# A decoder layer on one core: the last 12 steps' maxima sent by transfers, the rows of ones written by GpSimd, the heads turned by transposes, the last batch normalised out of the bank

## The reference

```python
x = _layernorm(x + attn(x))          # causal self-attention with folded low-rank weights
x = _layernorm(x + xattn(x, ctx))    # queries from x; keys and values from [ctx, x], causal over x
x = _layernorm(x + ffn(x))           # 128 -> 64 units, each with a 16-wide relu layer of its own -> 128
# in each attention, per head:
dots = q @ k.T / sqrt(8);  attn = softmax(where(mask, dots, -inf));  out = attn @ v
```

## Time and profile before

| | |
|---|---|
| median of 3 runs | 268.14 us (268.12 to 269.94) |
| profiled execution, its own time | 270.45 us |
| span of the profiled execution | 268.7 us |
| busy PE / DVE / ACT / POOL | 91% / 72% / 72% / 39% |
| mean granted TensorE clock | 0.937 of full |

### The profile page before, as it was taken

How to read it: one execution, slowest core, us unless ns; L and a number is a source line. 1 busy time by engine, 2 the same in 40 slices (tenths; PEclk the granted TensorE clock), 3 DMA queues, 4 the chain that set the end, 5 groups by cost and what they waited for, 6 DMA issues and landing times.

```text
span 268.7 us, 7856 instructions
## 1 busy us (share of the span) xinstructions
PE 243.7 (91%) x3037; PEld 150.3 (56%) x3037; DVE 193.8 (72%) x422; ACT 193.1 (72%) x412; POOL 106.0 (39%) x286
## 2 busy tenths in 40 slices
PE   8989998979999998899999999999999999998680
PEld 5676676758785654354555546544446455556440
DVE  1899991956868998979878897699878776544101
ACT  3263888867879786689987888789977987682131
POOL 7203597595745253721125222523321540412301
PEclk9997999979999997899999999999999997979757
DMA  4917888793997746370000000253000000000000
GB/s 103 372 60 146 245 143 122 241 175 58 285 157 155 115 133 104 118 119 3 4 0 2 2 0 4 91 104 47 2 0 2 23 2 0 5 20 2 20 0 20
DMA packets 20358, 21.53 MB, mean 80 GB/s; under 512 B 1185, under 2 KB 18017, under 8 KB 20193
## 3 DMA queue, kind: packets, MB, share of 16 engines
q1 hardware_dynamic: 20176, 20.90, 35.3%
q10 hardware_dynamic: 144, 0.13, 0.2%
HBM read 11.85 MB, written 9.18 MB: 78 GB/s over the span
## 4 chain that ended last, share of the span: by engine, by line
PE 56%; ACT 15%; DVE 13%; issue 8%; POOL 7%; ACTq 0%; POOLq 0%; DVEq 0%
PE psum L1200 15%; ACT probs L865 8%; PE psum L1157 8%; PE psum L1137 5%; PE psum L1124 5%; DVE pm L971 3%; PE psum L1292 2%; PE psum L1300 2%; PE psum L1140 2%; PE psum L1212 2%; DVE pm L973 2%; PE psum L1139 2%; ACT ctxT_sb L901 2%; PE psum L1060 2%; ACT qk L899 2%
## 5 line engine op out<-in xcount | busy, mean ns | idle before, releaser
L865 ACT ACTIVATE probs<-psum 128x512 f32<-128x512 f32 (+1 forms) x256 | 117.2, 571 | 11.1 <-PE psum L1157 9.5
L971 DVE TENSOR_REDUCE pm<-psum 128x1 f32<-128x512 f32 x128 | 79.3, 682 | 9.8 <-PE psum L1137 9.7
L973 DVE TENSOR_REDUCE pm<-psum 128x3 f32<-128x384 f32 x128 | 63.2, 549 | 8.9 <-PE psum L1124 8.6
L1200 PE MATMUL psum<-probs,v 128*9 128x256 f32 (+5 forms) x1024 | 64.9, 369 | 1.9 <-POOL probs L799 1.7
L899 ACT ACTIVATE qk<-psum 3x512 bf16<-3x512 f32 x64 | 37.4, 584 | 15.0 <-PE psum L1212 14.6
L1200 PEld LDWEIGHTS psum<-probs,v 128*9 128x9 f32 (+2 forms) x1024 | 28.1, 99 | 19.5 <-issue 5.8
L1137 PE MATMUL psum<-km,qk 51*128 51x512 bf16 x128 | 34.5, 388 | 1.2 <-ACT qk L899 0.4
L1157 PE MATMUL psum<-qk,km 51*128 51x256 bf16 x256 | 32.9, 272 | 1.9 <-ACT probs L865 0.7
L799 POOL TENSOR_SCALAR_AFFINE_SELECT probs<-probs 128x512 f32<-128x512 f32 x32 | 20.2, 639 | 33.0 <-ACT probs L865 33.0
L1157 PE MATMUL psum<-qk 51*128 51x256 bf16 (+1 forms) x256 | 32.1, 252 | 0.8 <-ACT probs L865 0.4
L1124 PE MATMUL psum<-neg,unit_b 64*128 64x256 bf16 (+1 forms) x256 | 32.0, 258 | 0.0
(11 more groups left out here) (117 smaller groups left out, 346.2 us busy)
## 6 DMA issues: line engine op xcount, KB each, us to landing
qk<-scr_qk SPq DMA_DIRECT2D x14, 384.0 KB, 6.9
km<-scr_m SPq DMA_DIRECT2D x8, 384.0 KB, 8.2
scr_qk<-spl SPq DMA_DIRECT2D x7, 384.0 KB, 2.6
scr_qk<-spl SPq DMA_DIRECT2D x21, 128.0 KB, 2.5
scr_m<-spl SPq DMA_DIRECT2D x4, 384.0 KB, 2.6
ctxT_sb<-ctxT SPq DMA_DIRECT2D x1, 1024.0 KB, 6.7
scr_m<-spl SPq DMA_DIRECT2D x4, 256.0 KB, 2.9
wb_sb<-wb SPq DMA_DIRECT2D x1, 642.0 KB, 4.6
```

What stands on the lines that cost most here:

```text
L865: nc.scalar.activation(probs[:, ring % PRING, r, 0:cols], bank_of(s)[:, 0:cols], ACT.Exp, scale=SCALE).then_inc(exp_done, 1)
L971: nc.vector.tensor_reduce(pm[:, place, 1 + 4 * qt:2 + 4 * qt], m, axis=AX.X, op=ALU.max).then_inc(reduced, 1)
L973: nc.vector.tensor_reduce(pm[:, place, 2:5], own_blocks(m), axis=AX.X, op=ALU.max).then_inc(reduced, 1)
L1200: last = nc.tensor.matmul(o, v[:, at:end], weights, start=(k == 0 and g in (0, NG - 1)), stop=(k == len(key_tiles(t)) - 1 and g >= NG - 2) ...
```

## The change

1. **Maxima of steps 20 to 31.** The shift uses two matmuls (all 12 rows, 128 columns each) in place of eight; ScalarE makes one activation of 12 x 256 into a new tile `shift_rows`; two transfers on SP's queue move six rows each into the queries, and T waits for these.
2. **Rows of ones.** For units 1 to 3 GpSimd writes the ones and zeros, behind the making of `spread` and ahead of its first step. For unit 0 a seventh matmul per pair (`edge`) adds the ones in PSUM, and one copy of 128 x 512 takes a pair out. `ones_bias` and its reduction go.
3. **Heads.** Two groups share each half of bank 7 (before: three and one), so a head has 8 slots of 9 columns where it had 10: the value tiles shrink from 360 to 288 columns. "norm" makes four 128 x 128 transposes; VectorE's multiply is two instructions.
4. **Last batch.** For wo and mo of batch 3 TensorE adds the residual into the bank (`add_rest`, ahead of its wait for yT or g), VectorE takes the moments from PSUM, GpSimd makes the factor only (two steps for four), VectorE applies it with two instructions.
5. **Planner.** Costs, ranks, `LATE`, `VALUES_AFTER` and the share of warm matmuls at the end are changed, so the order of all engines is a new one.

The diff at its core (the costs' unchanged entries and plain renamings are left out):

```diff
-VALUES_AFTER = (4, 6, 8)
+VALUES_AFTER = (1, 4, 6)
-VG, VJ = 3 * (HS + 1), 10 * (HS + 1)
+VG, VJ = 2 * (HS + 1), HG * 2 * (HS + 1)
-LATE = [(("qk", 0), 0), (("qk", 1), 0), (("qk", 2), 3), (("v1", 0), 0), (("qk", 3), 6), (("v1", 1), 0), (("m", 0), 2),
-        (("vm", 0), 13), (("m", 1), 4), (("vm", 1), 13), (("m", 2), 11), (("vm", 2), 11), (("m", 3), 25),
-        (("vm", 3), 23)]
+LATE = [(("qk", 0), 0), (("qk", 1), 0), (("qk", 2), 0), (("v1", 0), 2), (("qk", 3), 5), (("v1", 1), 0), (("m", 0), 9),
+        (("vm", 0), 10), (("m", 1), 10), (("vm", 1), 15), (("m", 2), 14), (("vm", 2), 22), (("m", 3), 15),
+        (("vm", 3), 26)]
...
-COST = {"start": 7500, "loaded": 13500, "s_ahead": 2200, "t_ahead": 2200, "slack": 60, "lat": 200, "switch": 110,
+COST = {"start": 9200, "loaded": 14000, "rep_hold": 200, "p_rep": 4.0, "p_qk": 0.5, "p_v2": 3.5, "p_norm": 0.0,
+        "s_ahead2": 2200, "t_ahead2": 1300, "s_ahead": 1300, "t_ahead": 800, "slack": 300, "lat": 200, "switch": 110,
+        "load": 90, "window": 0, "borrow": 400, "gap": 500, "fill": 115, "filled": 0.6, "filled_last": 0.85,
+        "gap_last": 250, "pv_soon": 300, "pv_few": 4, "pv_left": 3, "pv_hold": 0, "p_misc": 0.0, "p_late": 3.5,
+        "p_mlp": 2.2, "p_behind": 3.0, "p_pv": 0.5, "p_pv_on": 3.0, "p_row": 0.0, "p_switch": 0}
...
 def in_place(t):
-    return True
+    return t < 20
...
+def on_the_spot(s):
+    return s[0] in ("wo", "mo") and s[1] == UNIT_ORDER[-1] - B
...
+        def send_rows(engine, t):
+            g = group(t)
+            for r in range(2):
+                rows = PARTS * 2
+                dst = qk[HALF * r:HALF * r + PARTS, unit(t) % B, 2 * g:2 * g + 2, 0, :]
+                engine.dma_start(dst, shift_rows[rows * r:rows * (r + 1), t % ROWBUFS, :]).then_inc(rows_in[g], 16)
...
             for s in plan:
-                if s[0] == "put":
+                if s[0] == "rows":
+                    sem_, value = emptied(("shift", s[1]))
+                    sp.wait_ge(sem_, value)
+                    send_rows(sp, s[1])
...
+            nc.gpsimd.memset(edge_ones, 1.0).then_inc(spread_ready, 1)
+            nc.gpsimd.memset(edge.rearrange("p (r c) -> p r c", r=2)[:, :, 0:PARTS], 1.0 / STRIP).then_inc(spread_ready, 1)
...
+            for u in range(1, B):
+                ones_under(nc.gpsimd, qk[:, u, :, 1, :]).then_inc(qk_ones, 1)
+                zeros_under(nc.gpsimd, qk[:, u, :, 0, :]).then_inc(qk_ones, 1)
...
                     pool.wait_ge(var_ready, n + 1)
+                    if on_the_spot(s):
+                        nc.gpsimd.tensor_scalar_add(vpe[:, :], moments[:, :, 1], EPS).then_inc(pool_step, 1)
+                        steps += 1
+                        pool.wait_ge(pool_step, steps)
+                        nc.gpsimd.tensor_tensor(rstd[:, :], vpe[:, :], minus_half[:, :], ALU.pow).then_inc(rstd_ready, 1)
+                        if s[0] == "wo":
+                            add_bias("wo", s[1])
+                        continue
...
+                    elif what == "shift":
+                        t = s[1]
+                        if t >= ROWBUFS and not in_place(t - ROWBUFS):
+                            act.wait_ge(rows_in[group(t - ROWBUFS)], rows_landed(t - ROWBUFS))
+                        last = nc.scalar.activation(shift_rows[:, t % ROWBUFS, :], m[0:PARTS * HG, 0:T], ACT.Copy, scale=-1.0)
...
-                        act.wait_ge(bias_ready, 1)
-                        nc.scalar.activation(qk[:, 0, s[1], 0, :], m[:, 0:T], ACT.Copy)
-                        last = nc.scalar.activation(qk[:, 0, s[1], 1, :], m[:, T:], ACT.Identity, bias=ones_bias[:, 0:1])
+                        last = nc.scalar.activation(qk[:, 0, s[1]], m.rearrange("k (a t) -> k a t", a=2), ACT.Copy)
...
+                        for g in range(2):
+                            last = nc.vector.tensor_tensor(dst[:, :, :, g], o[:, :, :, g, 0:HS],
+                                                           sums[:, :, :, g].unsqueeze(3).to_broadcast([P, 2 * QT, HG, HS]), ALU.mult)
...
+                        if on_the_spot(s):
+                            res_free(s)
+                            rows = m[:, 0:QT * C].rearrange("p (n c) -> p n c", n=QT)
+                            row_moments(rows)
+                            dve.wait_ge(rstd_ready, n + 1)
+                            for i in range(QT):
+                                nc.vector.tensor_scalar(x1[:, b, i, :], rows[:, i, :], moments[:, i, 0:1], rstd[:, i:i + 1], ALU.subtract,
+                                                        ALU.mult).then_inc((dve_misc_done, applied[what])[i], 1)
+                            continue
...
+            def add_rest(s, m):
+                if on_the_spot(s):
+                    what, b = s[0:2]
+                    pe.wait_ge(*((x1b_ready, order_of["ln1"][("ln1", b)] + 1) if what == "wo"
+                                 else (x2b_ready, order_of["wo"][("wo", b)] + 1)))
+                    for i in range(QT):
+                        nc.tensor.matmul(m[:, i * C:(i + 1) * C], ident, x1b[:, b, i, :], start=(i == 0), stop=False,
+                                         skip_group_check=True)
...
-                            for n, cols in ((0, (NG - 1) * HG * (HS + 1)), (1, HG * (HS + 1))):
-                                o = m[:, qt * NH * (HS + 1) + n * (NG - 1) * HG * (HS + 1):][:, 0:cols]
-                                last = nc.tensor.matmul(o, headsT[:, at % 2, n, qt * P:(qt + 1) * P], used_rows[n], start=True,
-                                                        stop=True)
+                            for n in range(2):
+                                last = nc.tensor.transpose(m[:, (2 * qt + n) * P:(2 * qt + n + 1) * P],
+                                                           headsT[:, at % 2, n, qt * P:(qt + 1) * P], ident)
```

More of the change, by code:

```diff
@@ new lines @@
+PE_COST = {"pv": 430, "pv_half": 225, "shift": 220, "rep": 660, "norm": 500, "x1T": 300, "yT": 300, "x2T": 300, "qk": 880,
+           "m": 880, "v1": 900, "vm": 900, "v2": 450, "wo": 530, "s": 430, "hid": 500, "g": 950, "mo": 530}
+ACT_COST = {"T512": 477, "T256": 265, "shift": 264, "rep": 480, "drain": 480, "x1T": 264, "yT": 264, "x2T": 264, "qk": 480, "m": 480,
+            "v1": 480, "vm": 480, "v2": 264, "s": 430, "g": 430, "hid": 480, "maxima": 580, "apply": 530}
+DVE_COST = {"S512": 598, "S384": 465, "comb": 95, "rep": 600, "norm": 900, "x1T": 340, "yT": 340, "x2T": 340, "qk": 600, "m": 600,
@@ L329, in emit @@
                     end = run("dve", end, DVE_COST[what])
+            elif on_the_spot(s):
+                end = run("dve", end, DVE_COST["moments"])
+                end = run("dve", run("pool", end + 60, POOL_COST["pow"]) + 60, DVE_COST["apply"])
+                done[("apply",) + s[0:2]] = end + 60
             else:
@@ L339, in emit @@
                 chain.extend([("qk", B + n), ("v2", n)])
+            elif on_the_spot(s):
+                if what == "wo":
+                    done[("more", what, n)] = run("pool", end + 60, POOL_COST["after"])
+                    chain.append(("x2T", n))
             elif what in ("wo", "mo"):
@@ L367, in emit, with plan_has_pv @@
                 chain.append(("x1T" if s[1] == "ln1" else "x2T", s[2]))
+    def plan_has_pv():
+        return len(pv_order) > 0
     def fill(gap):
         k = min(range(FREE_BANKS), key=lambda k: (free_at[k], -k))
-        n = int(min(gap, 4000) * COST["filled"] // COST["fill"])
+        share = COST["filled"] if maxima or exps or not plan_has_pv() else COST["filled_last"]
+        n = int(min(gap, 4000) * share // COST["fill"])
         if free_at[k] <= free["pe"] and n:
@@ L423, in schedule @@
                 early = s[0] in MLP and s[1] < B - 1
-                best.append((start_of(s), COST["p_mlp" if early else "p_late" if s in LATE_STEP or s[0] == "rep" else "p_misc"], n, s))
+                hold = COST["rep_hold"] if s[0] == "rep" and s[1] // 2 > (group(step) if step < NG else NG) else 0
+                best.append((start_of(s) + hold, COST["p_mlp" if early else "p_late" if s in LATE_STEP else RANK.get(s[0], "p_misc")], n, s))
         if pvs:
@@ L450, in schedule @@
         gap = start_of(s) - now
-        if gap > COST["gap"]:
+        if gap > COST["gap" if maxima or exps else "gap_last"]:
             fill(gap)
@@ L590, in emptied, with rows_landed @@
                 return split_left, split_no[s] + 1
+            if on_the_spot(s):
+                return applied[s[0]], order_of[s[0]][s] + 1
             return (act_misc_done, act_no[s] + 1) if s in act_no else (dve_misc_done, dve_no[s] + 1)
+        applied = {"ln1": x1_ready, "wo": x2_ready, "mo": x3_ready}
+        def rows_landed(t):
+            return 32 * sum(1 for x in range(t + 1) if group(x) == group(t) and not in_place(x))
         def put_size(i):
@@ L824, in _ @@
                 elif s[0] == "apply" and s[1] != "mo":
[L825 to L831 removed]
+                    add_bias(s[1], s[2])
         @block.scalar
```

(7 more changed lines are left out.)

127 lines of the change are left out of this document (62 added, 65 removed).

## The result

The changed kernel takes 259.11 us (median of 4 runs, 254.71 to 264.63), beside 268.83 us for the kernel before in the same comparison. The ratio of undisturbed runs, those within 1.5% of the fastest of their kernel, is 0.948 (0.941 to 0.955). It flatters the change: the changed kernel's two such runs had mean clocks of 0.976 and 0.986, and when it was run again beside its variants (e5) the ratio was 0.980. In both kernels the time goes with how long TensorE's clock stands at 1.2 GHz in an execution: the kernel before took 265.2 us at a mean granted clock of 0.973 and 273.0 at 0.918.

The account below looks back on a forecast made before the run. TensorE was taken to pace 140 to 235 us, VectorE the start, a chain the end. Terms 2.5 + 0.3 + 4.0 + 2.8 + 1.1 - 1.5 = 9.2 us: 268.14 becomes 259.0 us (255 to 263).

Parts of the forecast that it names:

- The transfers and ScalarE's relief: Steps 20 to 31: ScalarE saves 7 to 9.3 us, worth 1.7 us (0 to 5) as TensorE sets the pace.
- TensorE's shifts: Last 12 steps: six of eight small matmuls go, 1.2 to 2.4 us of work, counted as 0.3 us gained.
- the late T: Each T ready 1.7 to 2.3 us later, paid once at the end: 1.5 us lost (0 to 2.3).
- One copy of 12 x 256: ScalarE's shift in the last 12 steps: one activation of 0.4 to 0.6 us replaces two.
- The slower rival: Steps 20 to 31: rows come late at every step, 272.6 us, up to 285; chance 0.10.
- The start: Earlier subtraction and spreading, fewer VectorE copies, earlier scores: 2.5 us gained (0 to 4).
- the cover that I named: Start: GpSimd's six memsets, 5.7 us, fall into 14.5 us of its waiting for first maxima, so cost 0.
- The norms: Heads: four transposes of 0.65 to 0.8 us replace matmuls of 1.05; seven units save 2.0 us (0 to 2.8).
- The last batch: Batch 3's end chain: norm 0.15 us, wo and mo 1.34 each; together 2.8 us gained (2.2 to 3.0).
- The clock at the end: Final slow-clock stretch: more warm matmuls in the gaps and a shorter chain gain 1.1 us (-1 to 3.8).
- The order: The planner's new order of all engines; the sum has no separate term for it.
- v2's tiles: Value tiles a fifth smaller, so less zeroing between two steps' splits: 0.3 us gained.

Follow-up runs that it names:

- e5: The changed kernel run again unaltered as its variants' reference: ratio 0.980 to the kernel before.
- e6: Changed kernel with two idle ScalarE activations behind each of the 12 shift copies: 263.9 us at like clock, 4.5 us more than the changed kernel.
- e7: Changed kernel with each step's rows sent through DRAM first: 263.0 us at like clock, 3.6 us more than the changed kernel.
- e10: Changed kernel with heads turned by plain fp32 matmuls on the identity, not transposes: 262.0 us at like clock, ratio 0.970 to the kernel before.
- e1: Changed kernel with rows in place, VectorE's ones, matmul norm and old last batch, new planner numbers kept: ratio 1.004, 268.8 us at like clock.
- e8: Changed kernel with the old planner numbers and without the row transfers: ratio 0.974 to the kernel before, 263.7 us at like clock.
- e3: Changed kernel without the row transfers, rows made in place by ScalarE, stages planned anew: ratio 0.989 to the kernel before, 264.0 us at like clock.
- e12: Changed kernel with unit 1's ones and zeros written by VectorE, units 2 and 3 by GpSimd: ratio 0.959, 257.7 us at like clock.

## Why the prediction was right, and where it wasn't

I said 259.0 us (9.2 off 268.14 is 258.9) and the median is 259.11. That it lies so close is luck: the four runs went from 254.7 to 264.6 us with their clocks. The sum without its clock term was a gain of 8.1 us, measured are 7.7 at like clock. The total is right, its parts are not: several terms were wrong by a factor, and they cancelled.

- **The transfers and ScalarE's relief** (1.7, and 0.3 of TensorE's shifts, less 1.5 for the late T: 0.5 together) was the step that failed. Removing them costs 4.6 (planned anew) to 6.4 us (same order). ScalarE's time was worth 0.37 of itself (e6), 3.6 us and not 1.7, and part of the rest lies in the PSUM bank that the shift's copy sets free earlier, which the sum didn't have. I argued that TensorE sets the pace at 91 of 95 us, so relief elsewhere gives little. But TensorE's fullness was no floor: from 120 to 210 us it is as busy in both kernels (86.7 and 87.6 us), while VectorE is busy for 9.2 us more, mostly with the steps' maxima. The steps' own matmuls add up to 114.3 us there for 106.8 (they overlap), the rest to 15.1 for 18.6: shifts and norms are shorter, less of other stages falls into the window, and the matmuls overlap more.
- **One copy of 12 x 256** took 0.36 us, below my 0.4 to 0.6. My half of the instruction's price was too careful.
- **The late T is paid once** (1.5) was right as against each step, but the 1.5 us don't show: TensorE waited for rows once, 0.4 us, as a T stands far behind its shift in the list. A further 1.3 us a step was hidden too, and only two long landings were paid (e7). The 2.0 us of fixed cost from the Trainium skill (DMA: Bandwidth & Descriptors, Anatomy of one DMA) stand there for transfers that GpSimd issues, and SyncE issues the ones here; e7's transfers of 6 KB mostly landed 1.3 us after their issue began.
- **The slower rival** didn't happen. SP sent the rows at once; its long waits were for the rows themselves. (In its sum the start, the norms and the last batch are 7.3 us, not 7.5.)
- **The start** (2.5): the first maximum came 2.26 us earlier, as said. The copies went otherwise than I had them: VectorE made one and not four, 0.69 us for 3.6, and ScalarE seven. And undoing GpSimd's memsets costs only 0.6 ± 1.1, and the cover that I named, GpSimd's idle time, wasn't the whole price. They were not free: they stretched VectorE's cast by 1.04 us.
- **The norms** (2.0): 2.6 ± 1.1 measured against e10's matmuls, which take 0.08 us a norm more than those of the kernel before; in that proportion 2.2.
- **The last batch** (2.8): the steps were right to 0.1 us (1.26 and 1.25 for 1.34 each), the gain was not. 0.6 ± 1.1 at like clock, 0.8 from drain to end in the two profiles. I took the chain's other stages as fixed, and the new order put batch 2's work into it. The overrun of warm matmuls and the residual's add, which I had as a lower bound of the clock's term, is there (0.9 us ahead of mo).
- **The clock at the end** (1.1): the slow stretch shrank from 9.9 us to about 4 (244.8 to 248.6) in the profiled executions. That is one execution of each, and no run takes this part alone. The mean clock was 0.949 in 39 runs before and 0.955 in 8 after, which by the slope would be 1.1 us, within the spread of the runs.
- **The order** I costed at nothing of its own. Alone it costs 1.7 us (e1); its worth is that with it the transfers' relief reaches VectorE.

The code parts other than the transfers give 3.4 us in the old order (e8) and 4.8 in the new one (e3 against e1, which both keep the single copies and the value tiles), where my terms for them add up to 7.6 with the 0.3 for v2's tiles.

## What to carry to other kernels

When three engines are at 80 to 95%, price relief on one by what stands behind its waits in the other queues: here a T that waited for the bank of the shift held back the scores that feed VectorE. A short copy out of PSUM gives its bank back earlier, besides the engine's time. And test a part together with its order, since the transfers were worth about 0 us in one order and 4.6 in the other. A chain at the end is only as short as what the planner puts into its gaps; shorten it and look at each gap again.

## What the runs showed of the hardware

- VectorE's cast of 128 x 512 from fp32 to bf16 took 0.43 us alone and 1.47 us beside GpSimd's memsets of 128 x 1024, and it ended 0.27 us behind the last of them (14.13 and 13.86 us). VectorE's own memsets of 128 x 1024 took 0.91 us beside GpSimd's memsets (e12), as in the kernel before. The subtractions of fp32 from PSUM (0.69 and 0.67) hardly changed. The Trainium skill (GPSIMD Engine Reference, Specifications) has GpSimd share its SBUF interfaces with VectorE, with contention for instructions that use two ports or two SBUF inputs; the trace fits it for this cast, though no row names the cast's ports, and the 1.04 us are its price.
- A transfer of 3 KB within the chip's core took SP about 0.7 us to issue, so a pair costs 1.4 us of SP's queue; I had taken 0.4 each from the store's 0.39. The write of 6 KB to DRAM mostly took 1.3 us from issue to landing, less than the store's 2.1, and at the longest 4.5, beside two transfers of 384 KB on the same queue; why is not shown.
- An activation out of PSUM took 0.36 us for 12 x 256 and 0.38 for 128 x 256, 0.58 for 3 x 512 and 0.60 for 128 x 512: the elements per partition set the time, and the partitions hardly count.
- The same kernel's mean granted clock varied from 0.931 to 0.986 between executions, and by the slope that is worth 10 us of 259.
